# Routed expert weights requested during the scatters, and the last down products ordered by output tile

## What is computed

```python
shared = einsum('ti,hi->th', silu(x @ sh_gate_w.T) * (x @ sh_up_w.T), sh_down_w)   # inner width 1408
probs  = softmax(x @ router_weight.T);  top_v, top_i = top_k(probs, 2);  top_v /= top_v.sum()
out = 0
for e in range(8):                                                                # inner width 352
    gate, up = split(x @ gate_up_proj[e].T)
    out += (silu(gate) * up @ down_proj[e].T) * combine[:, e:e+1]
out = out + sigmoid(x @ shared_gate_w.T) * shared
x = x + layernorm(out)
```

## Time and profile before

| | us |
|---|---|
| median of 3 runs (2018.06 to 2021.29) | 2019.19 |
| the profiled execution | 2018.83 |
| its span (first to last instruction) | 2016.8 |
| PE busy in it | 1941.4 (96%) |
| DVE, ACT, POOL busy | 1486.6, 1197.5, 797.8 |
| last layer: from 1352.6 to the end | 664 |

### The profile page before, as it was taken

One profiled execution on the slowest core, in us unless ns is written; L12 is line 12 of the kernel. 1 busy time (PEld: TensorE's weight loads), 2 busy tenths in 40 slices (PEclk: granted clock), 3 DMA queues, 4 the chain that ended last, 5 costly groups with the idle time before them and its releaser, 6 DMA issues. The chain is left out here.

```text
span 2016.8 us, 32105 instructions
## 1 busy us (share of the span) xinstructions
PE 1941.4 (96%) x10126; PEld 1648.5 (82%) x10126; DVE 1486.6 (74%) x3406; ACT 1197.5 (59%) x2977; POOL 797.8 (40%) x1206
## 2 busy tenths in 40 slices
PE   7999999989999999999999999989899999999997
PEld 5677777768888888888888888767788889888875
DVE  7788566687777777777777778976477778774665
ACT  6752222467666666666666667764376677674343
POOL 3342000685655555555555556862400000001552
PEclk9999999999999999999999999999999999999998
DMA  7344010227000000000000000134798899884563
GB/s 269 126 142 140 16 48 21 80 73 241 22 12 22 12 22 12 1 32 2 22 12 22 33 1 17 52 112 166 259 328 306 314 324 324 303 312 139 196 205 125
DMA packets 82518, 245.02 MB, mean 121 GB/s; under 512 B 10784, under 2 KB 11424, under 8 KB 80448
## 3 DMA queue, kind: packets, MB, share of 16 engines
q1 hardware_dynamic: 77232, 226.20, 32.7%
q0 software_dynamic: 5120, 16.78, 2.3%
HBM read 207.55 MB, written 45.61 MB: 126 GB/s over the span
## 5 line engine op out<-in xcount | busy, mean ns | idle before, releaser
L307 PE MATMUL l_xp<-att_w_hi,xT_hi 128*128 128x512 f32 x512 | 207.6, 405 | 4.8 <-ACT att_qkv L2433 4.3
L307 PE MATMUL l_xp<-att_w_hi,xT_lo 128*128 128x512 f32 x512 | 200.5, 392 | 0.0
L307 PE MATMUL l_xp<-att_w_lo,xT_hi 128*128 128x512 f32 x512 | 199.6, 390 | 0.0
L965 POOL TENSOR_SCALAR att_pr<-att_pr,rec_ri 128x384 f32<-128x384 f32 (+2 forms) x256 | 141.6, 565 | 125.5 <-DVE rec_ri L1633 121.8
L2462 ACT ACTIVATE att_pr<-att_pr,rec_nb,rec_r 128x384 f32<-128x384 f32 (+2 forms) x256 | 168.6, 662 | 36.1 <-DVE rec_nb L1604 35.3
L3908 POOL DMA_INDIRECT y<-moe_rows,moe_slotA x16 | 16.4, 1022 | 417.4 <-DMA moe_rows<-moe_lo_f 414.2
L969 POOL TENSOR_TENSOR att_rot<-att_rot,att_rot 128x384 f32<-128x384 f32 x128 | 129.8, 1014 | 107.1 <-DVE att_rot L1627 107.1
L1600 DVE CUSTOM_DVE_ANT_0 att_pr<-l_dd,att_mask 128x384 f32<-128x384 f32 (+2 forms) x256 | 119.1, 502 | 64.6 <-PE l_dd L307 59.8
L2433 ACT ACTIVATE att_qkv<-l_xp 128x512 f32<-128x512 f32 x128 | 76.3, 596 | 122.2 <-PE l_xp L307 113.4
L1638 DVE TENSOR_TENSOR att_pT_lo<-acc,att_pT_hi 128x768 fp32r<-128x768 f32 (+2 forms) x128 | 108.8, 850 | 27.0 <-ACT att_pT_hi L2455 26.8
L2455 ACT ACTIVATE att_pT_hi<-acc 128x768 fp32r<-128x768 f32 (+2 forms) x128 | 92.5, 722 | 44.3 <-PE acc L3236 23.2
(11 more groups left out here) (333 smaller groups left out, 6595.5 us busy)
## 6 DMA issues: line engine op xcount, KB each, us to landing
y<-in_moe_rt SPq DMA_DIRECT2D x59, 704.0 KB, 6.3
y<-in_moe_rt SPq DMA_DIRECT2D x39, 768.0 KB, 6.5
sraw_gu<-in_moe_sgu SPq DMA_DIRECT2D x44, 512.0 KB, 3.7
moe_sraw_d<-in_moe_sd SPq DMA_DIRECT2D x44, 256.0 KB, 4.4
moe_xs<-in_zeros SPq DMA_DIRECT2D x39, 256.0 KB, 6.3
moe_lo_f<-moe_xs SPq DMA_DIRECT2D x39, 256.0 KB, 6.7
moe_rows<-moe_lo_f SPq DMA_DIRECT2D x39, 256.0 KB, 6.6
att_raw_w<-in_qkv_w SPq DMA_DIRECT2D x8, 1024.0 KB, 4.8
```

Source lines behind the costliest of these rows:

```text
L307: mm = pe.matmul(out, lhsT, rhs, start=(i == 0), stop=(i == len(terms) - 1))
L965: pool.tensor_scalar(p, p, ri[:, j % 2, g:g + 1], 1.0, ALU.mult, ALU.mult).then_inc(sa("p"), 1)
```

## The change

Eight edits, all in the last layer:

1. `PRE_SHARED` is 13: R -1 comes after S 11 instead of S 10, and R 0 after S 12.
2. `load_pair(0)`, `load_pair(1)`, `load_pair(2)` and `load_rd(0)` move from R -1 to S 7, S 8, S 9 and S 10. Each waits for the scatters that read its part of `y` (the semaphore `scattered` becomes five, one for each three token tiles). R -1 keeps both `load_xs` and `load_pair(3)`.
3. On PE `shared_down(12)` moves out of S 13 into R 0, between `turn_xs(1)` and `turn_h(0)`. S 13 then has no down product.
4. DVE and ACT do R 39 (the last tile's hidden split and down-weight split) one S item earlier than PE (`splits_first`).
5. On ACT `shared_out` moves behind `sgu_split(n + 1)` and `sd_split(n)`.
6. The last three down products (chunks 41, 42, 43) are ordered by `LAST_DOWN`. Tile 0 of chunk 41 is done in S 42, everything else in S 43 behind its gate and up: tiles 0 and 1 are finished first, then tile 2, then tile 3. Chunk 43's operands get buffers of their own in the routed ring (`hs_of`, `sd_of`).
7. C 15 comes before S 43 instead of behind it.
8. POOL executes `drain` at C 12, and does the residual addition of tile 12 itself (`add_x(12)`, in F 13); DVE waits for all of POOL's `rstd_shift` and then adds tiles 13 to 15.

```diff
-PRE_SHARED = 12
+PRE_SHARED, RAW_FROM = 13, 7
+LAST_DOWN = [(N_SH - 3, 0), (N_SH - 2, 0), (N_SH - 3, 1), (N_SH - 2, 1), (N_SH - 1, 0), (N_SH - 1, 1)] + \
+    [(N_SH - 3 + j, t) for t in (2, 3) for j in range(3)]
...
-            share = -(-len(todo) // (left - k))
+            share = len(todo) if k == left - 2 else -(-len(todo) // (left - k))
...
+def splits_first(items):
+    out = list(items)
+    k = out.index(("R", RT_TILES))
+    out[k - 1], out[k] = out[k], out[k - 1]
+    return out
...
+                    if n == RAW_FROM:
+                        sp.wait_ge(s("owner"), 1)
+                        sp.wait_ge(s("scattered0"), 96)
+                        load_pair(0)
...
+                    elif n == RAW_FROM + 3:
+                        sp.wait_ge(s("scattered3"), 96)
+                        load_rd(0)
                 elif kind == "R" and n == -1:
-                    sp.wait_ge(s("owner"), 1)
-                    sp.wait_ge(s("scattered"), 32 * NT)
+                    sp.wait_ge(s("scattered4"), 128)
                     sp.wait_ge(s("s_up"), SH_CHUNKS)
                     load_xs(0)
-                    load_pair(0)
-                    load_pair(1)
-                    load_rd(0)
                     load_xs(1)
-                    load_pair(2)
                     load_pair(3)
...
+                    if n == CMB:
+                        pool.drain()
                 elif kind == "F":
                     if n < NT:
                         rstd_shift(n)
+                    if n == CMB + 1:
+                        add_x(CMB)
...
-                        for m in range(CMB, NT):
+                        dve.wait_ge(s("shift"), NT)
+                        for m in range(CMB + 1, NT):
                             last_add(m)
...
                 if kind == "S" and n < N_SH:
-                    if n % SH_CHUNKS == 1 and n > 1:
-                        shared_out(n // SH_CHUNKS - 1)
                     if n + 1 < N_SH:
                         sgu_split(n + 1)
                     sd_split(n)
+                    if n % SH_CHUNKS == 1 and n > 1:
+                        shared_out(n // SH_CHUNKS - 1)
...
-                    if n:
+                    if n == N_SH - 2:
+                        shared_down(n - 1, tiles=(0,))
+                    elif n == N_SH - 1:
+                        for j, t in LAST_DOWN[1:]:
+                            shared_down(j, tiles=(t,))
+                    elif n and n < N_SH and n != PRE_SHARED:
                         shared_down(n - 1)
...
+                    if n == 0:
+                        shared_down(PRE_SHARED - 1)
```

52 lines of the change are left out of this document (37 added, 15 removed).

## The result

The changed kernel ran in 2010.53 us (median of 5 runs, 2007.9 to 2013.33), beside 2020.22 us for the kernel before on the same chip (5 runs, 2018.06 to 2021.29). The ratio is 0.9955, with a 95% interval of 0.9944 to 0.9966: about 9.1 us less, between 6.9 and 11.3. The forecast was 11.8 less, 2007.4 us. So it is faster, the median lies at the upper edge of the range of 2004 to 2011, and the gain is smaller than I said.

What follows compares the result with a forecast made beforehand. PE, busy 96% of the span, bounds the kernel, so its pauses and the stretch behind its last matmul can be won: 7.3 + 1.6 + 0.55 + 0.6 + 1.65 = 11.7 us, giving 2007.4 us; range 2004.0 to 2011.0.

Steps and rivals of the forecast that it cites:

- The start: Start of the routed stage: waits of 2.6, 2.7, 1.5 and clock's 1.4 us go, 0.9 comes: 7.3 us gained.
- the overlap: At PE's pauses: each also loses 0.16 us of matmul overlap; five go, one comes, 0.6 us gained.
- DVE at that point: After S 11's up matmuls: DVE's splits finish by 8.7 us, `s_mul(12)` starts on time, the 2.7 us wait goes.
- SP should not stop: S 7 to S 10: scatters land before SP's weight requests need them, tiles 0 to 2 some 8 us ahead.
- rival (a): S 7 on: full DMA queues return up to 3 of 7.3 us, 2008.5 to 2010.5; chance 0.20 together with (b).
- untouched, ± 2: Routed stage: the other three token-tile waits, 2.0 us, are left alone; earlier start changes them by plus or minus 2.
- Edit 5 at n = 34: Chunk 34: splits ahead of ACT's copies let DVE multiply at 1923.4 instead of 1923.96, 0.55 us gained.
- The tail: From S 42's up matmuls to the last addition: two new pauses of 0.4, net gain 1.65 us.
- The drain: End of the kernel: POOL's early drain taken as 0, with up to 1 us possible from a shorter end.
- rival (e): Start of the routed stage: PE's 2.7 us stay because DVE's order made them: 2012 us, chance 0.04.
- (c): Routed stage and end: its own waits go too and the drain matters, 2004.4 to 2005.5 us; chance 0.14.
- (b): Chunk 12: ACT's copies delay the silu beyond the 1.6 us left, 2009 to 2010; chance 0.20 together with (a).

Runs made afterwards that it cites:

- the run with late weights: The changed kernel with the early weight requests undone, pairs 0 and 1 and the down block asked for behind the first token tile: 2009.34 us, ratio 0.9952.
- second trace: The changed kernel run once more without any edit, for another trace of it: 2008.2 us, ratio 0.9944 to the kernel before.

## Why the prediction was right or wrong

**The start, -7.3 and 0.3 of the overlap: right in size, wrong in cause.** Measured -7.75 and -8.00 (-7.9 from S 2), with the new pause of 0.9 where I had put it and the clock at 1.00. One term was counted wrong: the 13 matmul starts from 1462.90 to 1466.37 us have 12 distances between them, 1.92 us at the higher clock, so the lower clock had cost 1.55 us and not 1.39. The earlier trace rows also has three of its four places at the start of the stage, not four. The 2.6 us for the token tile I had put down to PE's coming a chunk later, and that stands. The step that failed is "DVE at that point: pair 0 split by 4.6 us after S 11's up matmuls", which gives the 2.7 us and the clock's 1.4 to the early weights. I had worked out that the chunk more delays PE, and used it for one wait only; asking for the weights at 1452.5 and needing them at 1466.1 was enough, and cost 0.3 us (the run with late weights). A term shared by two edits has to be worked out once with each edit alone.

**The scatters.** "SP should not stop" comes without cost in the changed kernel only because nothing there is in a hurry: in its second trace SP waits 0.8 us for the last scatter ahead of the token tile, and PE does not notice. I looked for the danger in the sum of the bytes (rival (a), 336 GB/s), and it lay in the order: at 337 GB/s the scatters were in time, and with one block issued ahead of the last two they were 3 us late.

**Edit 3: right.** 1.5 us gone and 0.93 new, measured 1.5 and 0.9.

**The routed stage, "untouched, ± 2": the term that was mis-sized.** Five waits of 5.3 us in the first trace, one of 0.5 in the second, and in others with the same order of loads in the routed items 3 of 3.5, 2 of 1.4, 2 of 1.3 and 2 of 1.1. I took the 2.0 us of the earlier trace rows for a property of the kernel; they are one draw of 0.5 to 5. Of the 6.4 us by which the first trace lies behind the second, this stage holds 6.1. I had named the cause ("a matter of queue position") and not the spread.

**Edit 4: right.** 1.86 us for 1.6 and the overlap.

**Edit 5 at n = 34: right by itself, and wrong in the sum.** Forecast -0.55, or -0.7 with the overlap. This is the step that made the gain smaller than forecast in both traces: the stretch S 29 to S 35 gained nothing and lost 2.4, because of a part of the change that I had put at nothing without a reason: edit 7's rule for the mixes and the thirteenth chunk in front leave 14 items for 16 tiles, and the first of them gets two. With the mixes spread the same stretch is 0.8 us under the kernel before, of which 0.74 are edit 5; what edit 5 does while S 29 is doubled has no run of its own. The order of the items shows it in one line, before any trace; I read edit 7 only at the end of the list, where it was meant to act.

**Edit 5 at n = 12:** I took 0, and no trace with the edit has a wait of PE there. The run with it undone has none for the product of chunk 12 either, only 0.4 us for a token tile.

**The tail: 1.65 forecast, 1.7 measured** up to the last addition (from S 42: 28.17 us before, 26.46 after). The last addition ends 5.9 us behind PE's last matmul, as forecast. POOL's three operations for the last tile:

```profile
2004.42 0.19 POOL L3949 TENSOR_SCALAR moe_ve<-moe_mv 128x1 f32<-128x1 f32 x1
2004.69 0.55 POOL L3951 TENSOR_TENSOR moe_rs<-moe_ve,moe_nhalf 128x1 f32<-128x1 f32 x1
2005.34 0.26 POOL L3953 TENSOR_SCALAR moe_sh<-moe_mv,moe_rs 128x1 f32<-128x1 f32 x1
```

1.18 us from 2004.42 to 2005.60, where the earlier trace rows had 2.31 beside three DVE additions: the 1.13 us came back whole, as the sum had it. The rule that the prediction cites from the Trainium skill ("SBUF — State Buffer", the shared port pair) agrees with that. Of the two pauses of 0.4 the first is 0.23 us of idle time and 0.16 of lost overlap, the forecast 0.4; at the second PE starts 0.54 us behind the matmul before it instead of 0.23, so it is 0.3.

**The drain: the step that failed is "I take 0, since POOL was idle from 2010.2 on already".** Idle is not finished: the end followed POOL by 6.6 us. The change gains 1.4 us behind the last addition, where I had allowed up to 1; 0.7 is the drain's, and 0.7 comes of POOL's being done earlier against the additions (4.2 instead of 4.9 without any drain).

**The total.** The lines sum to -12.6 us in the second trace and -6.2 in the first, around the forecast of -11.7. The comparison gave 9.1 (6.9 to 11.3) with the first five runs and 11.3 (8.7 to 14.1) with the second. That the sum came so near is luck in part: +3.1 us at S 29 to S 35 against -1.5 at the end and up to -1.9 in the routed stage. One slip in the chances: rival (e), at 2012 us, is 0.36% faster, so "faster by over 0.2%" should have had 0.96 and "within" 0.02. Of the rivals, (c) was right in its second half, and (b) named the right engine at the wrong chunk. Whether the first five runs had more token-tile waits than the second five can't be settled, since only one of each five has a trace.

## What to carry over

When two edits remove the same wait, cost it with each of them alone: one may be free to leave out, or harmful on its own. Where a rule shares out work over slots, write out the whole list for the new counts; a remainder moves to the other end of it. And ask for the small transfer that is needed first ahead of the large ones: one exchanged request took away waits of 2.0 us in the kernel before and of 0.5 and 5.3 in two executions of the changed one.

## What the runs showed of the hardware

- The program ended 6.5 to 6.6 us behind POOL's last instruction in three kernels whose stores lay differently, and a drain of POOL behind its last gather, in idle time, took 1.4 us (before) and 0.7 us (changed) off the end. With the drain the end lay 1.5 us behind the landing of the last store in fourteen traces; without it 2.1 to 2.9.
- A DVE subtraction of two SBUF operands stretched from 1.22 to 3.86 us beside two POOL additions of 1.3 us each, and another from 0.69 to 1.63 when the additions were moved there. In the first case the additions kept their usual time; in the second the first of them took 1.64, beside a DVE subtraction that had started 0.17 us ahead of it and kept its 0.69.
- The last scatter of 256 KB, queued by POOL, took 7.1 us to land with one 768 KB load of SP's issued 2.2 us ahead of it, and 4.0 in the kernel before. With that load moved away SP could go on 3.6 us earlier, though the 24 us ahead of it were as full (0.96 of the DMA time, 337 GB/s, against 0.95 and 328).
- Behind stops of PE of 3.71, 3.71 and 2.74 us the granted clock fell to the lower level, 1.2 GHz instead of 2.4, for part or all of the next 5 us (means of 0.66, 0.50 and 0.66), and the chunk behind took 1.6, 2.7 and 1.5 us longer. Behind stops of 0.4 to 2.0 us in the first trace of the changed kernel, and behind the one of 2.6 us in the kernel before, it stayed at 1.00 in the 4 to 5 us that follow.
